# VectorE takes over the output copies of unit 1 in the first network's steps, one core

## The chip, the cores and the metric

One core of a Trainium2 chip runs the whole program. The metric is the time in microseconds (us) from launch to end on the device; the median of several runs counts, and one execution is profiled. TensorE multiplies and transposes into PSUM, whose eight banks are `bank[0]` to `bank[7]` here, each 128 partitions by 512 float32. ScalarE (ACT in the profile) and VectorE (DVE) read PSUM and write SBUF; GpSimd (POOL) works in SBUF alone; SyncE (SP) issues transfers.

## The reference, cut to what matters

```
x = x + cross_attention_0(layernorm(x), ctx)        # 16 heads of 8
x = x + network_0(layernorm(x))                     # 6 layers, 16 heads of 64, windows of 32 tokens
x = x + cross_attention_1(layernorm(x), ctx)
x = x + network_1(layernorm(x))                     # 2 layers, 8 heads of 64, windows of 64 tokens
# one layer of network_0, for each of 16 batches of 128 tokens x 128:
h = shift_tokens(x);  q, k, v = split(h @ Wqkv)
q, k = l2norm(q) * qs, l2norm(k) * ks               # per head
q, k = rotate(q), rotate(k)                         # rotary tables, 8 * cos and sin
p = softmax(mask(q @ k.T));  x = x + (p @ v) @ Wo
x = x + (a * gelu(gate)) @ W2 + b2,   a, gate = split(norm(shift_tokens(x)) @ W1 + b1)
```

All of it is float32 but the mask, which is added in bfloat16.

## The kernel before

Each engine has one program written out by hand, and the engines meet at semaphores: `wait_ge(sem, n)` before an instruction, `then_inc(sem, 1)` behind it. An engine takes its instructions strictly in the order of its program, so one that waits holds up all behind it.

The first network is a pipeline of steps `s = 0 ... 98`. A batch of one layer (`p`, 0 to 95) is split in two units of 8 heads, `i = 0` and `i = 1`. `step_0(s)` exists once for every engine; it works on `p = s` (queries, keys, rotation, sums of squares), on `s - 1` (norm, turning q and k, scores of unit 0), on `s - 2` (softmax, values) and on `s - 3` (values of unit 1, projection by `wo`, residual). The feed-forward network works on groups of four batches and spreads over four steps, which I call by their counter c of `ff_phase`, (s - 7) mod 4: c = 0 mean, variance and the previous group's second matmul, c = 1 normalise and first gate matmul, c = 2 the other gate matmuls, with `ACT.Gelu` on ScalarE at the step's end, c = 3 the hidden matmuls.

What touches the change, in the order of one step:

- TensorE: `values_all(1, s-3)` (line 790) writes the attention output of unit 1 into banks 7 and 6 and increments `AT["o"][1]`. Then `keys(1, s)` and `queries(1, s)` (line 710, two matmul rows each) into banks 1 and 0. Then `project_out` (line 823, 16 rows) waits for `AT["oe"][1]`, reads `o_t[0]` and `o_t[1]` and writes bank 7. Later the values of unit 1 (`project_in(1, s-2, 2, 7, "v")`, line 710) overwrite bank 7 and wait for `AT["res"][0]`, the residual.
- ScalarE: after the squares of unit 0 and `turned(0, s-1, 0)` comes `outputs(1, s-3)`, two copies of 128x256 from banks 7 and 6 into `o_t[1]` (line 1609), then the exponents of unit 1 (line 1578). The same helper copies unit 0's output at the end of the step, before the next step's exponents of unit 0.
- VectorE: newton's last two operations (line 2180 writes `rnorm`), `rotate(0, s, 1)` and `rotate(0, s, 0)`, the reciprocals of the softmax sums, one feed-forward operation, two sums of squares (line 2136), `row_max_all(1, s-2)` (line 2195, two reductions), `rotate(1, s, 1)` and `rotate(1, s, 0)` (lines 2124 and 2129, three instructions each), `residual(0, s-3)` (line 2214), and so on until newton.

The words that tie them:

```
pe.wait_ge(AT["oe"][i], p + 1)         # project_out, for i in (0, 1)
at(pe, AT["res"][0], s - 2)            # before the values of unit 1 go to bank 7
dve.wait_ge(AT["k" if c else "q"], un(i, p))   # rotate: keys or queries are in the bank
```

Of the kernel before, what the change touches and what calls it, by code (L numbers as in the profile page):

```python
# [63 lines left out]
def build(nc, A, out):  # L64
# [9 lines left out]
    with ExitStack() as ctx:  # L74
        sb = lambda name, shape, dt=F32: ctx.enter_context(nc.sbuf_tensor(name, shape, dt))
        sem = lambda name: ctx.enter_context(nc.semaphore(name))
        bank = [ctx.enter_context(nc.psum_tensor(f"bank{i}", [P, BLK], F32)) for i in range(8)]
# [64 lines left out]
        o_t = [slot(34 + i) for i in range(2)]  # L142
# [38 lines left out]
        AT = {n: [sem(f"at_{n}{i}") for i in range(2)] for n in UNIT}  # L181
# [23 lines left out]
        def un(i, p):  # L205

            return 2 * p + i + 1
# [5 lines left out]
        def at(eng, sem_, n):  # L213

            if n > 0:
                eng.wait_ge(sem_, n)

        def ff_phase(ph, s):

            t = s - ph["lo"]  # L220
            first, steps, groups = (7, 4, 24) if ph["net"] == 0 else (5, 2, 8)
            if t < first:
                return -1, -1, -1
            g, c = divmod(t - first, steps)
            f = 4 * ph["layer0"] + g
            return c, f if g < groups else -1, f - 1 if 1 <= g <= groups else -1
# [87 lines left out]
        def g_square(act, n, k):  # L314

            act.wait_ge(LN["cen"], NBLK + n + 1)
            nc.scalar.activation(g_sq[n % 2], g_cen[n % 2], ACT.Square).then_inc(LN["sq"], 1)
# [1133 lines left out]
        def _(act):  # L1451
# [89 lines left out]
            def act_phase(ph):  # L1541
                lo, hi, ni = ph["lo"], ph["hi"], ph["net"]
                live = lambda p: lo <= p < hi

                def square(i, p, c):

                    act.wait_ge(AT["rk" if c else "rq"], un(i, p))
                    at(act, AT["ssk" if c else "ssq"], un(i, p - 1))
                    nc.scalar.activation(sq[i][c], bank[c][:], ACT.Square).then_inc(AT["sqk" if c else "sqq"], 1)  # L1549
# [20 lines left out]
                def exponents_all(i, p):  # L1570

                    at(act, AG["pt"][i][0], p - 1)
                    at(act, AG["ri"][i][0], p - 1)
                    for g in range(2):
                        act.wait_ge(AG["mx"][i][g], p + 1)
                        for j in range(4):
                            h = 2 * j + g
                            ins = nc.scalar.activation(pb[i][0][p % 2][:, h * DH:(h + 1) * DH], bank[3 + g][:, j * DH:(j + 1) * DH],  # L1578
                                                       ACT.Exp, bias=amx[p % 2][:, i, h:h + 1], accum_out=asum[p % 2][:, i, h:h + 1])
                        ins.then_inc(AG["ex"][i][g], 1)  # L1580

                def probs_all(i, p):

                    act.wait_ge(AG["pt"][i][0], p + 1)
                    at(act, AT["o"][i], p)
                    nc.scalar.activation(pbt[i][0], bank[5 + i][:], ACT.Copy).then_inc(AG["pte"][i][0], 1)
# [7 lines left out]
                def values(i, p):  # L1594

                    act.wait_ge(AT["v"][i], p + 1)
                    at(act, AT["o"][i], p)
                    nc.scalar.activation(v_s[i], bank[7][:], ACT.Copy).then_inc(AT["ve"][i], 1)
# [35 lines left out]
                def step_0(s):  # L1634
                    c, f, before = ff_phase(ph, s)
                    if live(s - 2):
                        exponents_all(0, s - 2)
                        values(0, s - 2)
                    if live(s - 3):
                        probs_all(1, s - 3)  # L1640
                    if live(s):
                        square(0, s, 1)
                        square(0, s, 0)
                    if s == 0:
                        gate_weights()
                    if live(s - 1):
                        turned(0, s - 1, 0)
                    if live(s - 3):
                        outputs(1, s - 3)
                    if s in (1, 3, 5):  # L1650
                        g_square(act, (s + 1) // 2, (s + 1) // 2)
                    if c == 0 and f >= 0:
                        ff_square(f)
                    if c == 1 and f >= 0:
                        ff_affine(f)
                    if live(s - 2):
                        exponents_all(1, s - 2)
                    if live(s):
                        square(1, s, 1)
                        square(1, s, 0)  # L1660
                    if live(s - 1):
                        turned(0, s - 1, 1)
                    if s == hi:
                        for k in range(2):
                            g_square(act, 4 + k, k)
                    if live(s - 2):
                        probs_all(0, s - 2)
                        values(1, s - 2)
                    if live(s - 1):
                        turned(1, s - 1, 1)  # L1670
                        turned(1, s - 1, 0)
                    if c == 2 and f >= 0:
                        ff_gelu(f)
                    if live(s - 2):
                        outputs(0, s - 2)
# [148 lines left out]
            t1, outputs = act_phase(PHASES[1])  # L1824
# [209 lines left out]
        def _(dve):  # L2034
# [76 lines left out]
            def dve_phase(ph):  # L2111
                lo, hi, ni = ph["lo"], ph["hi"], ph["net"]
                live = lambda p: lo <= p < hi

                def rotate(i, p, c):
# [15 lines left out]
                                                      ALU.mult)  # L2131
                    ins.then_inc(AT["rk" if c else "rq"], 1)

                def sum_squares(i, p, c):
                    dve.wait_ge(AT["sqk" if c else "sqq"], un(i, p))
                    nc.vector.tensor_reduce(ss[:, i, HU * c:HU * c + HU], heads(sq[i][c]), AX.X, ALU.add  # L2136
                                            ).then_inc(AT["ssk" if c else "ssq"], 1)
# [52 lines left out]
                def row_max_all(i, p):  # L2190

                    dve.wait_ge(AT["s"], un(i, p))
                    for g in range(2):
                        at(dve, AG["ex"][i][g], p - 1)
                        nc.vector.tensor_reduce(amx[p % 2][:, i, g:HU:2], bank[3 + g][:, 0:256].rearrange("p (j k) -> p j k", j=4),  # L2195
                                                AX.X, ALU.max, negate=True).then_inc(AG["mx"][i][g], 1)
# [130 lines left out]
                def step_0(s):  # L2327
                    if live(s - 1):
                        newton(s - 1, 9, 11)
                    if s == hi:  # L2330
                        outer(ph, 0)
                        outer(ph, 1)
                    if live(s):
                        rotate(0, s, 1)
                        rotate(0, s, 0)
                    if s == 0:
                        x_step(NB + 1)
                    if live(s - 2):
                        row_sum_all(0, s - 2)
                    feed_forward_0(s, 0)  # L2340
                    if live(s):
                        sum_squares(0, s, 1)
                        sum_squares(0, s, 0)
                    if live(s - 2):
                        row_max_all(1, s - 2)
                    if live(s):
                        rotate(1, s, 1)
                        rotate(1, s, 0)
                    if live(s - 3):
                        residual(0, s - 3)  # L2350
                    feed_forward_0(s, 1)
                    if s == hi:
                        for k in range(2):
                            g_centre(dve, 4 + k, k, k)
                    if s == hi + 1:
                        for k in range(2):
                            g_normalise(dve, 4 + k, k, k)
                    if live(s - 2):
                        row_sum_all(1, s - 2)
                    if live(s):  # L2360
                        sum_squares(1, s, 0)
                        sum_squares(1, s, 1)
                    feed_forward_0(s, 2)
                    if live(s):
                        newton(s, 0, 3)
                    if live(s - 1):
                        row_max_all(0, s - 1)
                    if live(s):
                        newton(s, 3, 6)
                        newton(s, 6, 9)  # L2370
                    if s == hi:
                        for k in range(2):
                            g_newton(dve, 4 + k, k, k)
# [324 lines left out]
```

## Time and profile before

| what | value |
|---|---|
| three runs | 2305.04 us median, 2299.03 to 2306.47 |
| profiled execution | 2299.02 us, span 2297.2 us, granted clock 0.987 |
| TensorE matmul busy | 2124.9 us, 93% of the span |
| VectorE busy | 1760.9 us, 77% |
| ScalarE busy | 1712.2 us, 75% |
| GpSimd busy | 1340.2 us, 58% |

The span runs from the first to the last instruction; the run's own time is 1.8 us longer. Busy time of TensorE counts matmul rows whose ends are modelled. The steps s = 7 to 94 of the first network fill 256 to 1765 us of the span.

### The profile page before, as it was taken

The numbers are of one execution on the slowest core, as the hardware profiler recorded it, in microseconds if no ns is written. First come the engines' busy times: TensorE is split into PE (matmuls) and PEld (weight loads), VectorE is DVE, ScalarE is ACT, GpSimd is POOL, SyncE is SP. The second block draws the span as 40 slices with busy tenths as digits, with TensorE's granted clock in tenths as the row PEclk, the third lists the DMA queues.
The fourth block names the chain that finished last, engine by engine and source line by source line (L and its number), as shares of the span: only waits on it lengthen the run. The fifth ranks groups of instructions, "written<-read, shape, count | busy, mean of one in ns | idle before, by whom it ended". The sixth has DMA issues, their size and how long they took to land. (4 is left out here: it accounts for less than half of the span.)

```text
span 2297.2 us, 88445 instructions
## 1 busy us (share of the span) xinstructions
PE 2124.9 (93%) x33790; PEld 1456.7 (63%) x33790; DVE 1760.9 (77%) x4953; ACT 1712.2 (75%) x5916; POOL 1340.2 (58%) x1270
## 2 busy tenths in 40 slices
PE   7988999999999999999999999999999886899997
PEld 5656666666666666666666666666666564666665
DVE  4988877778777878777778777877777478788873
ACT  3767788787787877787887777887788543778784
POOL 1337666666666666665676566666666124766660
PEclk8999999999999999999999999999999998999999
DMA  4001221112211222112211122111221100000001
GB/s 112 4 3 39 70 58 45 41 46 67 57 43 39 64 51 57 39 43 61 57 46 42 43 65 60 46 39 45 52 53 43 48 10 10 13 13 16 13 9 28
DMA packets 144799, 96.93 MB, mean 42 GB/s; under 512 B 61976, under 2 KB 137408, under 8 KB 144384
## 3 DMA queue, kind: packets, MB, share of 16 engines
q1 hardware_dynamic: 143232, 91.02, 15.5%
q8 instruction: 274, 4.49, 0.8%
q14 instruction: 141, 1.16, 0.2%
q10 hardware_dynamic: 1152, 0.26, 0.1%
HBM read 23.11 MB, written 1.05 MB: 11 GB/s over the span
## 5 line engine op out<-in xcount | busy, mean ns | idle before, releaser
L710 PE MATMUL bank<-wqkv,hs 128*128 128x512 f32 x1344 | 666.7, 614 | 19.3 <-ACT arena L1609 13.7
L1931 POOL TENSOR_TENSOR arena<-arena,rnorm 128x512 f32<-128x512 f32 x448 | 455.5, 1046 | 388.5 <-DVE rnorm L2180 387.3
L1924 POOL TENSOR_TENSOR arena<-arena 128x512 f32<-128x512 f32 x448 | 568.0, 1275 | 132.5 <-DVE arena L2129 132.2
L1578 ACT ACTIVATE arena<-bank,amx 128x64 f32<-128x64 f32 x1536 | 458.8, 336 | 8.5 <-DVE amx L2195 8.3
L2124 DVE TENSOR_TENSOR arena<-bank,rot 128x512 f32<-128x512 f32 x448 | 306.9, 685 | 82.7 <-PE bank L710 79.0
L1555 ACT ACTIVATE arena<-bank 128x512 f32<-128x512 f32 x448 | 264.4, 617 | 132.0 <-PE bank L731 130.9
L710 PEld LDWEIGHTS bank<-wqkv,hs 128*128 128x128 f32 x1344 | 228.6, 191 | 203.8 <-issue 154.9
L1578 ACT ACTIVATION_READ_ACCUMULATOR arena<-bank,amx 128x1 f32 x1536 | 352.3, 229 | 0.0
L2129 DVE TENSOR_TENSOR arena<-bank,rot 128x256 f32<-128x256 f32 x896 | 334.0, 414 | 0.0
L731 PEld LDWEIGHTS bank<-ident,arena 128*128 128x128 f32 x1792 | 212.6, 142 | 152.8 <-issue 128.3
L2136 DVE TENSOR_REDUCE ss<-arena 128x8 f32<-128x512 f32 x448 | 283.4, 670 | 32.5 <-ACT arena L1549 32.3
L1549 ACT ACTIVATE arena<-bank 128x512 f32<-128x512 f32 x448 | 265.9, 647 | 42.0 <-DVE arena L2129 41.2
L1938 POOL TENSOR_TENSOR arena<-arena,ainv 128x512 f32<-128x512 f32 x192 | 200.7, 1045 | 164.9 <-DVE ainv L2203 164.7
L731 PE MATMUL bank<-ident,arena 128*128 128x128 f32 x1792 | 251.5, 274 | 14.1 <-POOL arena L1931 6.4
L1609 ACT ACTIVATE arena<-bank 128x256 f32<-128x256 f32 x384 | 127.2, 387 | 174.6 <-PE bank L790 173.7
L823 PEld LDWEIGHTS bank<-arena,wo 128*128 128x128 f32 x1792 | 221.6, 194 | 55.1 <-issue 48.1
L790 PE MATMUL bank<-arena 64*64 64x32 f32 (+1 forms) x9216 | 186.1, 221 | 49.0 <-issue 47.6
L823 PE MATMUL bank<-arena,wo 128*128 128x128 f32 x1792 | 226.9, 279 | 3.0 <-ACT arena L1609 2.6
L790 PEld LDWEIGHTS bank<-arena 64*64 64x64 f32 x9216 | 160.6, 134 | 71.0 <-issue 54.5
L2195 DVE TENSOR_REDUCE amx<-bank 128x4 f32<-128x256 f32 x384 | 143.8, 416 | 39.8 <-PE bank L767 39.2
L767 PE MATMUL bank<-arena 64*32 64x64 f32 (+1 forms) x12288 | 168.8, 217 | 0.0
L767 PEld LDWEIGHTS bank<-arena 64*32 64x32 f32 x12288 | 154.9, 105 | 0.3
(213 smaller groups left out, 3229.8 us busy)
## 6 DMA issues: line engine op xcount, KB each, us to landing
arena<-arena SPq DMA_DIRECT2D x768, 64.0 KB
wqkv<-in_L_ffn_Wqkv_dram SPq DMA_DIRECT2D x24, 256.0 KB
hs<-z SPq DMA_DIRECT2D x128, 32.0 KB, 1.8
hs<-z SPq DMA_DIRECT2D x128, 31.8 KB, 1.9
fx<-z SPq DMA_DIRECT2D x31, 128.0 KB, 2.2
fx<-z SPq DMA_DIRECT2D x31, 127.0 KB, 2.5
wqkv<-in_L_ffn_Wqkv_dram SPq DMA_DIRECT2D x24, 128.0 KB
w<-in_L_ffn_W_dram SPq DMA_DIRECT2D x6, 341.0 KB
```

The source lines that it names most:

```text
L710: nc.tensor.matmul(bank[o][:], src[:], wqkv[w][:, off:off + 512], start=True, stop=True).then_inc(AT[name] if part < 2 else AT[name][i], 1)
L731: mm = nc.tensor.transpose(bank4[o][:, j, :], rc[i][c][p % 2][:, j * P:(j + 1) * P], ident[:])
L767: mm = nc.tensor.matmul(bank[3 + g][q:q + 32, DH * j:DH * j + n], q_t[i][rows, P * j + q:P * j + q + 32], k_t[i][rows, P * j + key:P * j + ...
L790: mm = nc.tensor.matmul(bank4[7 - half][to:to + DH, j, q0:q1], src[g][rows, DH * h:DH * h + DH], pbt[i][0][rows, h * P + q0:h * P + q1], s ...
L823: mm = nc.tensor.matmul(bank4[7][:, 0, :], wo[w][:, i, j, :] if ni == 0 else wo[w][:, j // 2, j % 2, :], o_t[i][:, j * P:(j + 1) * P], sta ...
L1549: nc.scalar.activation(sq[i][c], bank[c][:], ACT.Square).then_inc(AT["sqk" if c else "sqq"], 1)
L1578: ins = nc.scalar.activation(pb[i][0][p % 2][:, h * DH:(h + 1) * DH], bank[3 + g][:, j * DH:(j + 1) * DH], ACT.Exp, bias=amx[p % 2][:, i, ...
L1924: nc.gpsimd.tensor_tensor(t, t, rs[i][c], ALU.add).then_inc(AT["ak" if c else "aq"][i], 1)
L1931: nc.gpsimd.tensor_tensor(t, t, rnorm[p % 2][:, i, HU * c:HU * c + HU].unsqueeze(2).to_broadcast([P, HU, DH]), ALU.mult).then_inc(AT["mk" ...
L2124: nc.vector.tensor_tensor(heads(rc[i][c][p % 2]), src, r[:, 2 * c, :].unsqueeze(1).to_broadcast([P, HU, DH]), ALU.mult)
L2129: ins = nc.vector.tensor_tensor(dst, src[:, :, (1 - a) * hd:(2 - a) * hd], r[:, 2 * c + 1, a * hd:(a + 1) * hd].unsqueeze(1).to_broadcast( ...
L2136: nc.vector.tensor_reduce(ss[:, i, HU * c:HU * c + HU], heads(sq[i][c]), AX.X, ALU.add).then_inc(AT["ssk" if c else "ssq"], 1)
```

## The change

VectorE gets a new helper `outputs`, called in its `step_0` between the maxima and the rotation of unit 1, for steps before `hi` = 96. ScalarE leaves its two copies out in those steps and keeps them from step 96 on. Data, banks, matmuls and semaphores stay as they were; TensorE's program is the same.

```diff
@@ ScalarE, step_0 @@
                     if live(s - 1):
                         turned(0, s - 1, 0)
-                    if live(s - 3):
+                    if live(s - 3) and (s >= hi):
                         outputs(1, s - 3)
@@ VectorE, dve_phase @@
+                def outputs(p):
+
+                    dve.wait_ge(AT["o"][1], p + 1)
+                    at(dve, AT["y"][0], p)
+                    for part in range(2):
+                        ins = nc.vector.tensor_copy(o_t[1][:, 256 * part:256 * part + 256], bank[7 - part][:, 0:256])
+                    ins.then_inc(AT["oe"][1], 1)
+
@@ VectorE, step_0 @@
                     if live(s - 2):
                         row_max_all(1, s - 2)
+                    if live(s - 3) and s < hi:
+                        outputs(s - 3)
                     if live(s):
                         rotate(1, s, 1)
                         rotate(1, s, 0)
```

On VectorE, in a step with c = 1, before the change, from the second sum of squares to the residual (`bank1` and `bank0` hold keys and queries of unit 1, `at_` names are the semaphores waited for):

```order
L2136 TENSOR_REDUCE ss<-arena 128x8 [waits at_sqq]
L2195 TENSOR_REDUCE amx0<-bank3 128x4 [waits at_ex10,at_s]
L2195 TENSOR_REDUCE amx0<-bank4 128x4 [waits at_ex11]
L2124 TENSOR_TENSOR arena<-bank1,rot1 128x512 [waits at_ak1,at_kt1,at_k]
L2129 TENSOR_TENSOR arena<-bank1,rot1 128x8x32 x2
L2124 TENSOR_TENSOR arena<-bank0,rot1 128x512 [waits at_aq1,at_qt1,at_q]
L2129 TENSOR_TENSOR arena<-bank0,rot1 128x8x32 x2
L2214 TENSOR_TENSOR z<-bank7,z 128x128 [waits at_y0]
```

The same place of VectorE's program with the change (lines of the maxima are 2203 here, of the residual 2222):

```order
L2144 TENSOR_REDUCE ss<-arena 128x8 [waits at_sqq]
L2203 TENSOR_REDUCE amx0<-bank3 128x4 [waits at_ex10,at_s]
L2203 TENSOR_REDUCE amx0<-bank4 128x4 [waits at_ex11]
L2139 COPY arena<-bank7 128x256 [waits at_y0,at_o1]
L2139 COPY arena<-bank6 128x256
L2124 TENSOR_TENSOR arena<-bank1,rot1 128x512 [waits at_ak1,at_kt1,at_k]
L2129 TENSOR_TENSOR arena<-bank1,rot1 128x8x32 x2
L2124 TENSOR_TENSOR arena<-bank0,rot1 128x512 [waits at_aq1,at_qt1,at_q]
L2129 TENSOR_TENSOR arena<-bank0,rot1 128x8x32 x2
L2222 TENSOR_TENSOR z<-bank7,z 128x128 [waits at_y0]
```

Two copies stand between the maxima and the rotation, and six rotation instructions and the residual stand behind them.

On ScalarE, the same step before the change, from the squares of unit 0 to the exponents of unit 1:

```order
L1549 ACTIVATE arena<-bank1 128x512 [waits at_ssk,at_rk]
L1549 ACTIVATE arena<-bank0 128x512 [waits at_ssq,at_rq]
L1555 ACTIVATE arena<-bank5 128x512 [waits at_s,at_qt0]
L1609 ACTIVATE arena<-bank7 128x256 [waits at_y0,at_o1]
L1609 ACTIVATE arena<-bank6 128x256
L1624 ACTIVATE arena<-arena,lnp0 128x512 [waits ff_xn]
L1578 ACTIVATE arena,asum0<-bank3,amx0 128x64 [waits at_mx10,at_ri10,at_pt10]
```

And with it:

```order
L1549 ACTIVATE arena<-bank1 128x512 [waits at_ssk,at_rk]
L1549 ACTIVATE arena<-bank0 128x512 [waits at_ssq,at_rq]
L1555 ACTIVATE arena<-bank5 128x512 [waits at_s,at_qt0]
L1624 ACTIVATE arena<-arena,lnp0 128x512 [waits ff_xn]
L1578 ACTIVATE arena,asum0<-bank3,amx0 128x64 [waits at_mx10,at_ri10,at_pt10]
```

The two copies and their wait for `at_o1` are gone from between the turned queries and the feed-forward operation.

## Rows read from the trace of the kernel before

**Rows 1.** Page, part 1: busy us, share of the span, instructions

```profile
PE 2124.9 (93%) x33790; PEld 1456.7 (63%) x33790; DVE 1760.9 (77%) x4953; ACT 1712.2 (75%) x5916; POOL 1340.2 (58%) x1270
```

**Rows 2.** Busy by engine from 256 to 1765 us: PE, PEld, DVE, ACT, POOL, PEclk

```profile
256.00:1765.00 1509.00, 1428.99 (x26397) 984.11 (x26397) 1180.93 (x3429) 1203.42 (x4385) 977.51 (x915) 1.00 0.20 50
```

**Rows 3.** Waits of PE, same stretch: us in total, times, longest us

```profile
PE bank L790 <- issue: 41.4, 62, 1.8
PE bank L761 <- issue: 19.4, 22, 1.0
PE bank L710 <- ACT arena L1609: 12.9, 15, 0.9
```

**Rows 4.** Timeline of step 80 (c = 1): start us, us, engine line, [idle before]

```profile
1514.36 0.66 ACT L1609 ACTIVATE arena<-bank 128x256 f32<-128x256 f32 x2 [0.21 <-PE bank L790]
...
1514.79 0.75 DVE L2195 TENSOR_REDUCE amx<-bank 128x4 f32<-128x256 f32 x2
...
1515.45 0.68 DVE L2124 TENSOR_TENSOR arena<-bank,rot 128x512 f32<-128x512 f32 x1
1515.61 0.19 PEld L823 LDWEIGHTS bank<-arena,wo 128*128 128x128 f32 x1 [0.24 <-issue]
...
1516.04 1.95 PE L823 MATMUL bank<-arena,wo 128*128 128x128 f32 x16
...
1518.03 0.29 DVE L2214 TENSOR_TENSOR z<-bank,z 128x128 f32<-128x128 f32 x1
...
1518.59 0.30 PEld L710 LDWEIGHTS bank<-wqkv,hs 128*128 128x128 f32 x2
1518.70 1.02 PE L710 MATMUL bank<-wqkv,hs 128*128 128x512 f32 x2
```

**Rows 5.** Timeline of step 78 (c = 3)

```profile
1480.85 0.74 DVE L2195 TENSOR_REDUCE amx<-bank 128x4 f32<-128x256 f32 x2
...
1481.61 0.19 PEld L823 LDWEIGHTS bank<-arena,wo 128*128 128x128 f32 x1 [0.24 <-issue]
...
1482.04 1.95 PE L823 MATMUL bank<-arena,wo 128*128 128x128 f32 x16
...
1484.03 0.28 DVE L2214 TENSOR_TENSOR z<-bank,z 128x128 f32<-128x128 f32 x1
...
1485.45 0.30 PEld L710 LDWEIGHTS bank<-wqkv,hs 128*128 128x128 f32 x2
```

**Rows 6.** Timeline of step 79 (c = 0)

```profile
1496.00 0.74 DVE L2195 TENSOR_REDUCE amx<-bank 128x4 f32<-128x256 f32 x2
1497.45 0.69 DVE L2124 TENSOR_TENSOR arena<-bank,rot 128x512 f32<-128x512 f32 x1 [0.71 <-PE bank L710]
...
1497.68 0.19 PEld L823 LDWEIGHTS bank<-arena,wo 128*128 128x128 f32 x1 [0.24 <-issue]
```

**Rows 7.** Groups of DVE by shape, 256 to 1765 us: count, busy us, mean ns

```profile
L2129 DVE TENSOR_TENSOR arena<-bank,rot 128x256 f32<-128x256 f32 x704 | 262.4, 414 | 0.0
...
L2252 DVE COPY arena<-bank 128x512 f32<-128x512 f32 x44 | 29.5, 670 | 8.6 <-PE bank L859 8.6
```

**Rows 8.** Timeline of step 78's start: PE released by a copy of ScalarE

```profile
1473.73 0.63 ACT L1609 ACTIVATE arena<-bank 128x256 f32<-128x256 f32 x2
...
1474.41 1.13 PE L710 MATMUL bank<-wqkv,hs 128*128 128x512 f32 x2 [0.86 <-ACT arena L1609]
```

**Rows 9.** Timeline of ACT, step 81 (c = 2), before the Gelu

```profile
1534.57 0.60 ACT L1555 ACTIVATE arena<-bank 128x512 f32<-128x512 f32 x1 [0.69 <-PE bank L731]
```

**Rows 10.** Timeline of steps 8 and 94, first and last of the stretch

```profile
278.67 0.74 DVE L2195 TENSOR_REDUCE amx<-bank 128x4 f32<-128x256 f32 x2
...
279.47 0.19 PEld L823 LDWEIGHTS bank<-arena,wo 128*128 128x128 f32 x1 [0.24 <-issue]
...
1754.57 0.74 DVE L2195 TENSOR_REDUCE amx<-bank 128x4 f32<-128x256 f32 x2
...
1755.34 0.19 PEld L823 LDWEIGHTS bank<-arena,wo 128*128 128x128 f32 x1 [0.24 <-issue]
```

## The prediction, made before the changed kernel had run

> **What bounds the kernel now.** I read the page's busy line first, to see which engine has no room. TensorE is busy for 93% of the span, VectorE 77% and ScalarE 75% [rows 1]. Then the windows: over the first network's steps TensorE is busy for 1428.99 of 1509.00 us at full clock, with 1180.93 for VectorE and 1203.42 for ScalarE [rows 2]. Only about 80 us are left in which TensorE does nothing, so the next question is who makes it wait. The waits answer it: 41.4 us inside the values matmuls and 19.4 us before the masks end with "issue", and 12.9 us end with ScalarE's output copy [rows 3]. Line 790 has no semaphore between its rows, so its stalls are of TensorE's own instruction stream. The 22 waits at line 761 and the 15 at line 710 come in steps with c = 3, behind the Gelu. Two of these three groups are therefore the only idle time that a lighter ScalarE could give back, and everything else that delays a TensorE instruction is paid in full.
>
> **What the change removes.** It takes 93 pairs of copies from ScalarE, 0.66 us a pair [rows 4]. Does anyone wait for that? The relief would have to reach the Gelu at the end of a step with c = 2, since what TensorE waits for comes behind it. Between the copy and the Gelu stands line 1555, before which ScalarE is idle for 0.69 us, until TensorE has turned the keys [rows 9]. I see such an idle time in each of the steps with c = 2 that I looked through (eight, from step 9 to 93). Freed time becomes more of that idle time. I count the removal as 0; the cover is TensorE's own order, and if it were gone the gain would be at most 0.66 us in each of 22 steps.
>
> **What it adds to VectorE.** Two copies of 128x256 out of PSUM. The nearest row is line 2129: the same shape, 414 ns each, the two of a pair 0.75 us from first start to last end [rows 7, 4]. The first of such a pair begins 0.34 us ahead of the second (0.75 less 0.41). The copy of 128x512 takes 670 ns [rows 7], less than two of the half size. So I take 0.66 us for what follows on VectorE and 0.75 us until `AT["oe"][1]` is incremented. Lower bound: the one copy of double width, 0.67 us, less the 0.09 by which the next instruction overlaps (the maxima end at 1515.54, the rotation starts at 1515.45 [rows 4]): 0.58. Upper bound: two of 414 ns without overlap, 0.82.
>
> **Where it lies beside other work.** In a step with c = 0 (and, from the same reading, c = 2), the maxima end at 1496.74, and the rotation starts 0.71 us later because it waits for the keys [rows 6]. Copies of 0.66 us fit. They end at 1496.66 + 0.75 = 1497.41, and TensorE loads `wo` at 1497.68: 0.2 us to spare. Cost 0.
>
> In a step with c = 1 or 3 VectorE is late: the maxima end at 1515.54 (1514.79 + 0.75) and the rotation starts at once, at 1515.45 [rows 4]. ScalarE had begun to copy at 1514.36, so the output has long been ready. Now the copies start at 1515.45 and end at 1516.20. TensorE wants to load `wo` at 1515.61 and to multiply at 1516.04. How a release that is late is paid is shown by [rows 8]: copies end at 1474.36, the next matmul row starts at 1474.41, and the pair takes 1.13 us instead of the 1.02 of [rows 4]. So 0.05 us for the semaphore and 0.11 us of an uncovered weight load. The projection effectively starts at 1516.20 + 0.16 = 1516.36 instead of 1516.04: 0.32 us late. For c = 3: the maxima end at 1481.59, the copies at 1482.26, the start moves to 1482.42 instead of 1482.04: 0.38 us [rows 5].
>
> **What is late next.** Behind the copies on VectorE stand both rotations and the residual, which TensorE needs before it puts the next values into bank 7. For c = 1: from the first rotation to the residual it is 2.58 us (1515.45 to 1518.03), of which the last 0.05 may be the projection's own end (1516.04 + 1.95 = 1517.99), so 2.53. From 1516.11 on that gives 1518.64, and 0.29 for the residual 1518.93, plus 0.16: the values start at 1519.09 instead of 1518.70 [rows 4]. That is 0.39 us, which contains the 0.32, not in addition. For c = 3 the residual ended at 1484.31 and the values are loaded at 1485.45 [rows 5], so 0.66 us more is hidden. The squares, sums and newton behind it follow TensorE again: the next gate copy waits for its matmul in any case. TensorE's delay moves the next step as a whole, and nothing later in it catches up.
>
> **How many steps.** I compared the end of the maxima with the load of `wo` in all steps from 4 to 95. The pattern of the rows above holds from step 8 (279.41 against 279.47) to step 94 (1755.31 against 1755.34) [rows 10]: 17 steps with c = 3, and 14 with c = 1 in which the residual comes out 0.4 to 0.5 us late (mean 0.45), and steps 4 and 6 like them. In the other 5 and 8 TensorE was itself late, mostly by a stall of its instructions, and the copies find room.
>
> Sum: 17 x 0.38 = 6.5, 14 x 0.45 = 6.3, 2 x 0.45 = 0.9: 13.7 us, say 14. Against the profiled execution's own time, 2299.02, that is 2313. The three runs have their median 6 us above that execution and their mean at 2303.5; I put the 14 us on the mean and forecast 2317 us. With the lower bound (0.58, 0.08 less in 33 steps) it is 11 us, with the upper (0.82, 0.16 more) 19.
>
> **A rule beside a row.** The row of line 2129 shows that the second of two instructions without a wait between them starts before the first has ended, 0.34 us after its start [rows 4, 7]. The Trainium skill ("VectorE: DVE Perf Modes", "The DRAIN you can't avoid") says that the next operation does not start until the pipe is empty, while its section on two Vector instructions with no wait between them lets one that is not held start earlier; its cost table gives 120 + 256 cycles at 0.96 GHz for one copy out of PSUM, 0.39 us, 0.78 for two. By the first rule with that price each of 33 steps would lose 0.12 us more and the sum would be an estimated 18 us. The rows decide for the overlap.
>
> **Rivals.**
> 1. *The copies are hidden* (0 to 6 us, about 2304). If TensorE's stalls of "issue" [rows 3] run on their own time, waiting 0.4 us earlier in a step lets its instructions arrive, and the stall shrinks by as much. For it: 41.4 us of such stalls, one in every second step. Against it: they come several us away from the projection. To bring 14 us under 6, over half would have to be absorbed.
> 2. *ScalarE's relief decides* (faster, about 2293). Place: the Gelu at the end of c = 2. ScalarE loses the copies and the idle time in front of them, 0.66 + 0.21 = 0.87 us in [rows 4]. If the 0.69 us of [rows 9] were ScalarE's own lateness seen through TensorE, the Gelu would start earlier by that much, and the 32.3 us of waits behind it [rows 3] would shrink by 22 x 0.87 = 19 us, at most by all 32. Against it: the idle time before line 1555 in every such step. It decides from 14 / 22 = 0.64 us a step on; 19 to 32 us back against 14 lost gives 2299 to 2285.
> 3. *The margin of c = 0 and 2 goes too.* It is 0.2 us. If a copy takes 0.6 us instead of 0.41 (two banks, the wait on `AT["o"][1]`), the pair costs 1.1, 0.44 more: 33 steps lose 0.44 more, and the 44 others 0.2: 14 + 14.5 + 9 = 37 us, 2341. Nothing in the rows speaks for it but that no such pair stands in them.
>
> **Chances.** Forecast (10 to 20 us more) 0.70; rival 1 0.17; rival 2 0.06; rival 3 0.07. About 0.3%, 7 us, is what a measurement of this kernel can tell from no change. The range 2302 to 2331 leaves out rival 2, most of rival 3 and the lower part of rival 1; the forecast's own is 2309 to 2325. Slower is the forecast and rival 3, 0.77; within 0.3% rival 1, 0.17; faster 0.06.
>
> **What would show it.** In the profile after: ACT's line 1609 falls from 384 to 198 rows; DVE has 186 copies of 128x256 near 0.41 us; a new line in TensorE's waits, the projection or its weight load released by VectorE's copy, about 0.3 us each in some 30 steps, and the values of unit 1 released by the residual with c = 1; steps with c = 1 and 3 longer by 0.4 us, the others unchanged; ScalarE's idle time before line 1555 with c = 2 still there. I am wrong if the step lengths with c = 1 and 3 stay (rival 1), if the waits behind the Gelu shrink (rival 2) or if the steps with c = 0 and 2 grow (rival 3).

## The result: 13 us slower, and where the profile shows it

| what | before | with the change |
|---|---|---|
| six runs each, median | 2302.77 us (2299.03 to 2306.47) | 2315.49 us (2312.96 to 2323.08) |
| profiled execution | 2299.02 us, span 2297.2 us, clock 0.987 | 2314.1 us, span 2311.8 us, clock 0.987 |

The ratio is 1.0061, 95% interval 1.0047 to 1.0075: 11 to 17 us, 14 by the ratio and 13 by the medians. The forecast was 2317.

The busy line of the page with the change, against [rows 1]:

```profile
PE 2132.2 (92%) x33790; PEld 1450.2 (63%) x33790; DVE 1824.2 (79%) x5139; ACT 1670.9 (72%) x5730; POOL 1340.3 (58%) x1270
```

VectorE has 186 instructions more and 63 us more work, ScalarE 186 fewer and 41 us less. TensorE's count is the same, and it is the engine that the time follows. What it waits for in the first network's steps (256 to 1780 us; us in total, times, longest), against [rows 3]:

```profile
PE bank L790 <- issue: 41.6, 59, 2.1
PE bank L761 <- issue: 18.9, 22, 1.0
PE bank L710 <- ACT arena L1609: 12.8, 15, 0.9
PE bank L823 <- DVE arena L2139: 6.2, 29, 0.6
```

The three old groups stand where they stood. One is new: the projection waits 29 times for VectorE's copy. The other sign that the prediction named for c = 1, the values of unit 1 released by the residual, is not there: neither TensorE's matmuls nor its weight loads have a row that ends with line 2222 in this stretch. What ScalarE waits for in the same stretch is the other half of the story:

```profile
ACT arena L1555 <- PE bank L731: 121.9, 133, 2.4
ACT arena L1609 <- PE bank L790: 84.0, 65, 2.4
ACT arena L1549 <- DVE arena L2129: 77.9, 126, 2.3
ACT arena L1578 <- DVE amx L2203: 58.9, 88, 1.2
```

Before, the same view (256 to 1765 us) had these rows:

```profile
ACT arena L1609 <- PE bank L790: 156.0, 131, 4.3
ACT arena L1555 <- PE bank L731: 117.7, 133, 2.2
...
ACT arena L1549 <- DVE arena L2129: 14.4, 43, 1.1
ACT arena L1578 <- DVE amx L2195: 4.5, 18, 0.5
```

ScalarE no longer waits 72 us for unit 1's values; it waits 64 us more for the rotated keys and queries and 54 us more for the maxima. So here ScalarE, which follows the others, does not get further when work is taken from it; it waits at the next place. Part of these waits is due to VectorE, which now comes 0.66 us later; e6 below shows the relief alone.

The steps themselves. Step 78 (c = 3) with the change; start us, duration us, engine and line, idle time before and its releaser in brackets; compare [rows 5]:

```profile
1493.58 0.74 DVE L2203 TENSOR_REDUCE amx<-bank 128x4 f32<-128x256 f32 x2
...
1494.24 0.74 DVE L2139 COPY arena<-bank 128x256 f32<-128x256 f32 x2
...
1494.90 0.68 DVE L2124 TENSOR_TENSOR arena<-bank,rot 128x512 f32<-128x512 f32 x1
1495.09 1.86 PEld L823 LDWEIGHTS bank<-arena,wo 128*128 128x128 f32 x16 [0.99 <-DVE arena L2139]
1495.12 2.02 PE L823 MATMUL bank<-arena,wo 128*128 128x128 f32 x16 [0.20 <-DVE arena L2139]
...
1497.42 0.28 DVE L2222 TENSOR_TENSOR z<-bank,z 128x128 f32<-128x128 f32 x1
...
1498.61 0.30 PEld L710 LDWEIGHTS bank<-wqkv,hs 128*128 128x128 f32 x2
```

From the start of the maxima to the projection it was 1482.04 - 1480.85 = 1.19 us and is 1495.12 - 1493.58 = 1.54: 0.35 later. The projection itself is 0.07 longer (2.02 for 1.95); its first weights are now loaded 0.03 before it, where before they were loaded 0.43 ahead, beneath an earlier matmul. Note that the wait in brackets says only 0.20 us for these 0.42. The list of waits above (6.2 us in 29 times) therefore understates what the release costs; the distance between two instructions tells it. The residual is early in both (1484.03 before the load at 1485.45; 1497.42 before 1498.61).

Step 80 (c = 1), against [rows 4]:

```profile
1527.95 0.74 DVE L2203 TENSOR_REDUCE amx<-bank 128x4 f32<-128x256 f32 x2
...
1528.61 0.75 DVE L2139 COPY arena<-bank 128x256 f32<-128x256 f32 x2
...
1529.27 0.68 DVE L2124 TENSOR_TENSOR arena<-bank,rot 128x512 f32<-128x512 f32 x1
...
1529.47 1.86 PEld L823 LDWEIGHTS bank<-arena,wo 128*128 128x128 f32 x16 [0.93 <-DVE arena L2139]
1529.50 2.02 PE L823 MATMUL bank<-arena,wo 128*128 128x128 f32 x16
...
1531.79 0.28 DVE L2222 TENSOR_TENSOR z<-bank,z 128x128 f32<-128x128 f32 x1
...
1532.12 0.30 PEld L710 LDWEIGHTS bank<-wqkv,hs 128*128 128x128 f32 x2
1532.23 1.02 PE L710 MATMUL bank<-wqkv,hs 128*128 128x512 f32 x2
```

From maxima to projection 1.25 us before, 1.55 now; from maxima to residual 3.24 and 3.84; from maxima to the values' matmul 3.91 and 4.28, 0.37 later. These 0.37 are the projection's: it starts 0.30 later and is 0.07 longer, and from its end to the values' matmul it is 0.71 us both times (1517.99 to 1518.70, 1531.52 to 1532.23), two groups of transposes without a gap. The residual ends at 1532.07, 0.05 before the values' weights are loaded. Its release has used up its margin but holds nothing up.

Step 79 (c = 0), against [rows 6]:

```profile
1509.89 0.74 DVE L2139 COPY arena<-bank 128x256 f32<-128x256 f32 x2
...
1510.62 0.69 DVE L2124 TENSOR_TENSOR arena<-bank,rot 128x512 f32<-128x512 f32 x1
1510.85 0.19 PEld L823 LDWEIGHTS bank<-arena,wo 128*128 128x128 f32 x1 [0.24 <-DVE arena L2139]
...
1511.28 1.95 PE L823 MATMUL bank<-arena,wo 128*128 128x128 f32 x16
```

The copies end at 1510.63, 0.22 us before the load, and load and matmul stand 0.43 apart, as in [rows 4]. The bracket names VectorE's copy, but its 0.24 us is the same idle time that "issue" ended before: the last releaser of a wait isn't always its reason.

I took a step's length as the time from its first rotation to the next step's. From steps 7 to 94, 22 of each c, the median change is +0.33 us with c = 1, +0.44 with c = 3, and 0.00 and 0.01 with c = 0 and 2. Steps 4 and 6 are 0.90 and 0.96 longer, but in the profile with the change the clock stood at its lower level at the end of step 6 (granted clock 0.96 over that step, 1.00 in the one before). At full clock step 6 is only about 0.2 longer.

### The profile page after: what moved, and what is told of

The parts are those of the page before. It is cut to its first block and busy times, and to the rows that moved or that the text cites. A ratio compares the mean times of both kernels' runs of the same rounds, so it can differ in the third digit from the quotient of the medians.

```text
span 2311.8 us, 88445 instructions
## 1 busy us (share of the span) xinstructions
PE 2132.2 (92%) x33790; PEld 1450.2 (63%) x33790; DVE 1824.2 (79%) x5139; ACT 1670.9 (72%) x5730; POOL 1340.3 (58%) x1270
## 5 line engine op out<-in xcount | busy, mean ns | idle before, releaser
L710 PE MATMUL bank<-wqkv,hs 128*128 128x512 f32 x1344 | 673.6, 620 | 19.2 <-ACT arena L1609 13.6
L1555 ACT ACTIVATE arena<-bank 128x512 f32<-128x512 f32 x448 | 262.5, 613 | 135.5 <-PE bank L731 134.3
L1549 ACT ACTIVATE arena<-bank 128x512 f32<-128x512 f32 x448 | 270.8, 634 | 107.3 <-DVE arena L2129 107.3
L1578 ACT ACTIVATION_READ_ACCUMULATOR arena<-bank,amx 128x1 f32 x1536 | 341.9, 223 | 0.0
L1598 ACT ACTIVATE arena<-bank 128x512 f32<-128x512 f32 x224 | 139.5, 623 | 18.6 <-PE bank L710 18.4
```

The source lines that it names most:

```text
L710: nc.tensor.matmul(bank[o][:], src[:], wqkv[w][:, off:off + 512], start=True, stop=True).then_inc(AT[name] if part < 2 else AT[name][i], 1)
```

## The experiments

Each was timed beside the kernel before on its own chip. **Time at full clock** below is the mean over the runs of a kernel of span x granted clock. TensorE bounds this kernel, so this is about what it would take if the clock never fell. It is my estimate from two numbers of each run, and it spreads less (standard error 0.4 to 0.9 us) than the times do (1.0 to 2.8 us).

| run | ratio to before, 95% | median us, this / before | at full clock, us over before | clock, this / before |
|---|---|---|---|---|
| e1_odd_steps | 1.0002 (0.9987 to 1.0018) | 2303.97 / 2301.26 | +0.5 | 0.9849 / 0.9850 |
| e2_even_steps | 1.0056 (1.0034 to 1.0078) | 2316.67 / 2301.26 | +12.9 | 0.9848 / 0.9850 |
| e3_before_maxima | 1.0057 (1.0036 to 1.0077) | 2315.15 / 2301.26 | +11.0 | 0.9840 / 0.9850 |
| e4_added_work | 1.0147 (1.0124 to 1.017) | 2337.2 / 2301.26 | +28.6 | 0.9828 / 0.9850 |
| e5_after_key_rotation | 1.0623 (1.0588 to 1.0658) | 2446.68 / 2301.79 | +139.9 | 0.9840 / 0.9852 |
| e6_light_scalare | 0.9997 (0.9979 to 1.0014) | 2301.44 / 2301.79 | -1.1 | 0.9850 / 0.9852 |
| e7_unit0_on_vectore | 0.997 (0.9955 to 0.9985) | 2296.7 / 2301.79 | -12.7 | 0.9822 / 0.9852 |
| e8_reductions_after_maxima | 1.0047 (1.0026 to 1.0068) | 2316.5 / 2302.23 | +4.9 | 0.9819 / 0.9848 |
| e9_reductions_before_maxima | 1.0053 (1.003 to 1.0075) | 2315.42 / 2302.23 | +6.2 | 0.9828 / 0.9848 |

The kernel with the change has 2279.5 us at full clock, against 2265.7 for the kernel before as timed beside e1 to e4, on another chip: +13.8. (The clocks of the kernel before beside the change itself are not on record.)

**e1_odd_steps and e2_even_steps: which steps pay.** e1 keeps VectorE's copies only in steps with odd s (c = 0 and 2), e2 only in those with even s (c = 1 and 3).

```diff
@@ e1, against the changed kernel; e2 has the parities the other way @@
-                    if live(s - 3) and (s >= hi):
+                    if live(s - 3) and (s >= hi or s % 2 == 0):
                         outputs(1, s - 3)
...
-                    if live(s - 3) and s < hi:
+                    if live(s - 3) and s < hi and s % 2 == 1:
                         outputs(s - 3)
```

> VectorE makes unit 1's output copies only in odd steps (c = 0 and 2), ScalarE in even ones. Theory A (the loss is the late release of the projection and, with c = 1, of the residual, in steps where VectorE has no idle time before the rotation): all of the loss is gone, same as before within 3 us (about 2303). Theory C (the copies cost in any step, through contention or longer work of VectorE): about half of the 13 us stays, 2309.

> VectorE makes the copies only in even steps (c = 1 and 3). Theory A: the whole loss, 12 to 15 us over before, about 2316. Theory C: half of it, about 2309.

e1 takes the time of the kernel before, e2 that of the whole change. e2's median steps are +0.33 (c = 1) and +0.44 (c = 3), the others 0.00 and -0.02. So the 44 or so pairs with c = 0 and 2 are free, and the cost is all in the other half. e1 tells one thing more: in its steps with c = 2 ScalarE is rid of the two copies and of the wait in front of them, at no cost elsewhere, and the waits behind the Gelu stay as they were (18.7 and 12.9 us in its list, 19.4 and 12.9 in [rows 3]). That is the test of rival 2 in its own place.

**e3_before_maxima: release early, residual late.** The copies move in front of the maxima. They end earlier, so the projection isn't held up, but everything behind stays 0.66 us late.

```diff
@@ against the changed kernel, VectorE, step_0 @@
-                    if live(s - 2):
-                        row_max_all(1, s - 2)
                     if live(s - 3) and s < hi:
                         outputs(s - 3)
+                    if live(s - 2):
+                        row_max_all(1, s - 2)
```

> All copies on VectorE, but ahead of the maxima, so that they end some 0.66 us earlier while the rotation and all behind it are as late as in the changed kernel. Theory A: the projection is released in time; only the residual with c = 1 stays late, 14 steps by 0.4 us, 5 to 7 us over before (2309). Theory B (VectorE's lateness as such costs, through squares, sums and newton): the whole 13 us stays, 2316. The waits of the projection for VectorE should be nearly gone in A.

The matmuls' wait for VectorE's copy is gone from the list. 30 weight loads still wait for it, but the projection starts 1.75 us behind the end of line 790's matmuls in the median step of each c, as in the kernel before, so they cost nothing. Yet the run is 11 us over before, not 5 to 7. That was a miss, and left a question: do late maxima cost something, or do the copies? See e9.

**e4_added_work: the delay without the copies, in the wrong size.** ScalarE keeps its copies, and VectorE gets two unused products in their place.

```diff
@@ against the kernel before, VectorE, step_0, between row_max_all(1, s - 2) and rotate(1, s, 1) @@
+                    if live(s - 3) and s < hi:
+                        for part in range(2):
+                            nc.vector.tensor_tensor(spare[:, part], rot_c[0][:], rot_c[1][:], ALU.mult)
```

> The kernel before, ScalarE keeps all copies, and VectorE makes two unused products of 128x256 in SBUF (about 0.7 us) between the maxima and the rotation. Theory A: no late projection, only the late residual with c = 1, 5 to 7 us over before (2309). Theory B: 13 us (2316). If ScalarE's relief was worth something in the changed kernel, this one is slower than that.

Far above both theories. The group of these products on VectorE (count | busy us, mean ns | idle before), and two pairs of them in the timeline, the second (step 80) with GpSimd beside it, say why (lines are one higher here):

```profile
L2349 DVE TENSOR_TENSOR spare<-rot_c 128x256 f32<-128x256 f32 x174 | 143.9, 866 | 0.0
```

```profile
1510.13 0.75 DVE L2349 TENSOR_TENSOR spare<-rot_c 128x256 f32<-128x256 f32 x2
...
1544.41 1.84 DVE L2349 TENSOR_TENSOR spare<-rot_c 128x256 f32<-128x256 f32 x2
1544.75 1.22 POOL L1939 TENSOR_TENSOR arena<-arena,ainv 128x512 f32<-128x512 f32 x1
1545.93 1.46 POOL L1925 TENSOR_TENSOR arena<-arena 128x512 f32<-128x512 f32 x1
```

While GpSimd was idle a pair took 0.75 us, beside a running GpSimd instruction 1.84. In the median step a pair took 0.75 us with c = 3 and 1.92 us with c = 0, 1 and 2. So the dose was the 0.66 us of the change in steps with c = 3, and nearly three times that in the others. The Trainium skill ("SBUF — State Buffer", "Who interferes with whom") says that a VectorE instruction with two SBUF inputs contends with a GpSimd instruction that reads SBUF, and that such contention is an exclusive lock. This trace agrees with it, 1.84 beside 0.75 us.

What the run still tells is where such a delay is paid. With c = 3, where the dose was right, the median step is +0.04 us, against +0.44 with the change: VectorE's lateness without the late release costs nothing there. With c = 0 and 2 even the large dose is free (0.00 and +0.01). With c = 1 it is +1.51. TensorE's waits name the place, line 711 being the matmul of the values of unit 1 into bank 7 and line 2215 the residual:

```profile
PE bank L711 <- DVE z L2215: 19.7, 16, 1.4
```

**e8_reductions_after_maxima and e9_reductions_before_maxima: the right size.** A reduction with one input from SBUF takes the place of the product; e8 puts the two behind the maxima, e9 in front.

```diff
@@ e8, against e4; e9 has the three lines ahead of row_max_all(1, s - 2) @@
-                            nc.vector.tensor_tensor(spare[:, part], rot_c[0][:], rot_c[1][:], ALU.mult)
+                            nc.vector.tensor_reduce(spare[:, part], rot_c[0][:], AX.X, ALU.max)
```

> The kernel before with two unused reductions of 128x256 (of a table in SBUF, one input) on VectorE between the maxima and the rotation of unit 1, in the steps where the change puts its copies; ScalarE keeps its copies. The reductions stand where the two products of the run with added work stood, but a reduction of this shape takes about 0.42 us as the maxima do, a pair 0.74 us, so this is the dose of the change, 0.66 us. Theory A (two releases): the projection waits for ScalarE and starts in time, so c = 3 costs nothing; with c = 1 the residual is late by what the change makes it, 0.3 to 0.4 us: 14 to 17 steps, 5 to 7 us in all. Rival B (VectorE's lateness as such costs a step, through maxima, squares and newton too): 13 us, in c = 1 and c = 3 alike. Rival C (the work that ScalarE keeps has to be counted as well): over 13 us.

> As the run before in this call, but the two reductions stand in front of the maxima of unit 1 instead of behind them. This repeats on VectorE what the run with the copies before the maxima did, without moving any copy. That run was 12 to 13 us over the kernel before where theory A gave 5 to 7. If late maxima are the reason (the exponents of unit 1 on ScalarE start later, and with them the transposes and values of unit 1), this run is 10 to 13 us over the kernel before and the one with the reductions behind the maxima 5 to 7. If the reason lies with the copies themselves (their wait for the values of unit 1 holds up maxima and rotation in some steps), both runs are equal within 3 us, at 5 to 7.

In e8 the dose is right. Step 76 (c = 1) with reductions, projection, residual and the values' matmul (line 711), and, below it, the group:

```profile
1457.66 0.73 DVE L2349 TENSOR_REDUCE spare<-rot_c 128x4 f32<-128x256 f32 x2
1457.80 0.19 PEld L824 LDWEIGHTS bank<-arena,wo 128*128 128x128 f32 x1 [0.24 <-issue]
...
1458.23 1.95 PE L824 MATMUL bank<-arena,wo 128*128 128x128 f32 x16
...
1460.83 0.28 DVE L2215 TENSOR_TENSOR z<-bank,z 128x128 f32<-128x128 f32 x1
...
1461.16 0.30 PEld L711 LDWEIGHTS bank<-wqkv,hs 128*128 128x128 f32 x2 [0.35 <-DVE z L2215]
1461.16 1.12 PE L711 MATMUL bank<-wqkv,hs 128*128 128x512 f32 x2
```

```profile
L2349 DVE TENSOR_REDUCE spare<-rot_c 128x4 f32<-128x256 f32 x176 | 64.6, 408 | 0.0
```

The projection starts in time, released by ScalarE, and now the residual is what TensorE waits for: from the projection's end (1460.18) to the values' matmul it is 0.98 us in place of 0.71. The median step is +0.32 us with c = 1 and +0.09 with c = 3, and the time at full clock is +4.9 us: theory A in place and size. By the clock on the wall it is 11 us over before (1.0047, interval 6 to 16 us), which the 13 us of rival B would fit as well; what speaks for A are the steps and the time at full clock. The rest is the granted clock, 0.9819 on the mean of 12 runs against 0.9848 in 20: 0.0029 x 2300 = 7 us. e9 equals e8 within the errors, at full clock as well (+6.2). So late maxima are not what made e3 dear; the 5 us between e3 and e9 go with the copies themselves, as e9's expectation had it. In e3 VectorE is seen to wait for the values before its copies, and maxima and rotation stand behind that wait:

```profile
DVE arena L2139 <- PE bank L790: 37.2, 54, 1.7
```

That this wait makes the whole 5 us is argued, not shown. Beside it stands that e3's list has 45.9 us of stalls at line 790, 4.5 more than before (e8 43.4, e9 44.6), and no run tells the two apart.

**e5_after_key_rotation: the release later still.** The copies move behind `rotate(1, s, 1)`.

```diff
@@ against the changed kernel, VectorE, step_0 @@
+                    if live(s):
+                        rotate(1, s, 1)
                     if live(s - 3) and s < hi:
                         outputs(s - 3)
                     if live(s):
-                        rotate(1, s, 1)
                         rotate(1, s, 0)
```

> All copies on VectorE, behind the rotation of the keys of unit 1, 1.27 us later than in the changed kernel. Theory A: each us by which the projection is released late costs a us in every step: about 1.6 us in 31 steps with c = 1 and 3, 1.5 us in the 59 others, 140 us over before (2440, 2400 to 2460). Theory B: VectorE's program is as long as in the changed kernel, so about 2316.

Measured +145 us. Every step pays, +1.58, 1.63, 1.56 and 1.69 us for c = 0 to 3, and the wait has grown:

```profile
PE bank L823 <- DVE arena L2139: 114.1, 87, 1.8
```

The projection's release is thus a hard edge. Once the 0.2 us of margin with c = 0 and 2 are used up, each step pays the delay in full.

**e6_light_scalare: what ScalarE's relief is worth.** The kernel before, with ScalarE's two copies cut to one of 8 columns. The wait for the values of unit 1 in front of the copy stays, and two thirds of the 0.66 us go.

```diff
@@ against the kernel before, ScalarE, outputs @@
-                    if ni == 0:
+                    if ni == 0 and i == 1 and 2 <= p < 93:
+                        nc.scalar.activation(o_t[1][:, 0:8], bank[7][:, 0:8], ACT.Copy).then_inc(AT["oe"][1], 1)
+                    elif ni == 0:
```

> The kernel before with ScalarE copying only 8 columns of one bank for unit 1, in place of two copies of 256 columns (batches 2 to 92 of the pipeline), so that most of unit 1's attention output is left out of the projection: ScalarE's relief alone, about 0.45 us a step. Theory A: no gain, 2303 within 3 us, because ScalarE waits for TensorE before line 1555. Rival (the relief counts): up to 10 us faster, 2293.

Ratio 0.9997, and at full clock -1.1 us with a standard error of 0.8. Relief of this copy is worth nothing that can be told from zero. Where the freed time went, with VectorE's program as it was (against the list of before above, line 1608 being the small copy):

```profile
ACT arena L1555 <- PE bank L731: 126.5, 134, 2.4
ACT arena L1611 <- PE bank L790: 83.6, 65, 2.2
ACT arena L1608 <- PE bank L790: 67.7, 63, 2.5
ACT arena L1549 <- DVE arena L2131: 30.0, 51, 1.1
...
ACT arena L1578 <- DVE amx L2197: 14.3, 26, 0.7
```

It is 9 us more before line 1555, 16 more for the rotations and 10 more for the maxima.

**e7_unit0_on_vectore: the copy for which TensorE does wait.** [rows 3] has 12.9 us of waits for ScalarE's copy, and [rows 8] shows one: unit 0's, behind the Gelu. This kernel leaves unit 1's copies with ScalarE and gives VectorE unit 0's, in steps with c = 2 only, in the idle time between newton's operations.

```diff
@@ against the kernel before; ScalarE, end of step_0 @@
-                    if live(s - 2):
+                    if live(s - 2) and not (c == 2 and f >= 0):
...
@@ VectorE, between newton(s, 3, 6) and newton(s, 6, 9); outputs_0 is as outputs, of unit 0 @@
+                    if live(s - 2) and c == 2 and f >= 0:
+                        outputs_0(s - 2)
```

> The kernel before, but in the 24 steps with c = 2 the output copies of unit 0 behind the Gelu go to VectorE, between two thirds of newton. If the waits at lines 710 and 761 with c = 3 come from ScalarE's chain behind the Gelu, they shrink by the 0.63 us of the copies: 22 to 24 steps, 13 us faster, about 2290. If VectorE's later newton holds up the norm on GpSimd and the turned queries, the gain is eaten, 2300 to 2305.

It is faster than both kernels: 2296.7 us in 12 runs, ratio 0.997. The waits of 12.9 us have become 0.8, while those before the masks grew from 19.4 to 25.0 (some of the gain meets the next late thing):

```profile
PE bank L790 <- issue: 40.3, 64, 2.0
PE bank L761 <- issue: 25.0, 19, 1.6
PE bank L731 <- POOL arena L1931: 4.8, 15, 0.8
PE bank L710 <- issue: 1.2, 2, 1.0
PE bank L710 <- ACT arena L1609: 0.8, 1, 0.8
```

VectorE has room for the pair here:

```profile
1533.11 0.76 DVE L2139 COPY arena<-bank 128x256 f32<-128x256 f32 x2 [0.71 <-PE bank L790]
```

At full clock it gains 12.7 us, the 13 expected. On the wall it gains 5 to 7, less than expected (2290), since its granted clock is 0.9822 against 0.9852.

## Why the prediction came out right

**Removal counted as 0.** Right. e1 shows it in the steps with c = 2, wait included, and e6 shows most of it alone in all steps. The lists of ScalarE's waits show where the freed time went: not only into the idle time before line 1555, as I wrote (9 us in e6, 4 with the change), but mostly into waits for rotations and maxima. The 0.69 us before line 1555 of [rows 9] is 0.45 in the same step with the change. Still there, and by e1 rival 2 had nothing to win.

**Price of the pair.** 0.66 us to the next instruction and 0.74 to 0.75 to the release: in step 78 they start at 1494.24 and the rotation at 1494.90. The mean of one copy is 413 ns in 186. The overlap that [rows 4, 7] showed for line 2129 holds for copies too. By the rule of the Trainium skill ("VectorE: DVE Perf Modes", "The DRAIN you can't avoid") without overlap the sum was 18 us. The 0.66 us from the first copy to the rotation, under two times 0.413, decide against it here; the total of 14 alone would not, since it came together partly by luck, as follows.

**c = 0 and 2 free.** Right, by e1 and by 0.22 us of margin left in step 79; e5 shows what lies beyond it.

**c = 3, 17 x 0.38.** The mechanism is right (e2 against e8: the median +0.44 becomes +0.09 once ScalarE releases). The term was a little small, 0.44 for 0.38. In step 78 it is 0.42: the copies end at 1494.98 and the projection starts 0.14 later, for which I had 0.05, and it is 0.07 longer, for which I had 0.11.

**c = 1, 14 x 0.45.** Here the number is near and the mechanism is half right. I let the residual decide (0.39 in step 80, with the projection's 0.32 inside it). Measured are 0.37 in step 80, all of it the late and longer projection; in none of the 22 steps is there a gap between it and the values' matmul. The residual arrives just in time, and the wait for it that I had named as a sign did not come. Alone it would cost nearly as much: in e8, where the projection is in time, the median step is +0.32, against +0.33 in the change. Before the change it had 0.33 us of margin (it ended at 1518.32, the values' matmul began at 1518.70, and a release takes 0.05), and 0.66 less 0.33 is what e8 pays; e4 pays 1.83 less 0.33 = 1.5. So the two releases run out together, and to repair only one of them would gain little in these steps, as e3 shows (+0.39).

**Steps 4 and 6, 0.45 each.** I had no closer reading of them than "like the others". At full clock they cost 0.90 and about 0.2, together 1.1 for 0.9, in one execution of each kernel.

The sum of all step lengths at full clock (each step's length less half of the time that the clock spent at its lower level, from one profile of each kernel) is 13.8 us longer from step 0 to 95: 9.3 with c = 3, where I had 6.5; 4.8 with c = 1, where I had 6.3; 1.3 less with c = 0, 0.0 with c = 2, and 1.0 in steps 0 to 6. 18 steps with c = 3 and 13 with c = 1 are over 0.2 us longer, for the 17 and 14 that I had counted. Such sums scatter by the stalls of TensorE's instructions: in e1, where nothing is to be seen, the four differ from before by -1.5 to +1.3 us. So the count of steps is borne out, c = 3 was sized too small, and that the forecast sum of 13.7 came so near is partly luck. By the profiles' own clock the same stretch is 18.9 us longer; 5 us of this is TensorE's clock, at its lower level for 24 us of it with the change and for 14 before.

**Rival 1** (stalls absorb the delay) fell: 41.4 us of issue stalls at line 790 before, 41.6 after. **Rival 3** fell with e1.

## What to carry to other kernels

Ask of an operation that is to move who waits for its release, and who waits for what will stand behind it, and price both in every kind of step: the same two copies cost nothing in half of the steps and 0.33 to 0.44 us in the others. Where two releases run out at the same time, a list of waits names only one of them, and an experiment that restores the other alone shows the second. Relief of an engine that itself waits in every step was worth nothing here; look in TensorE's waits for the one copy that it waits for (here unit 0's behind the Gelu) and move that one. To measure a suspected delay, fill it with an instruction whose duration is known in that place, not with one that may compete with another engine.

## What the runs showed of the hardware that I had not expected

- The same VectorE product of two SBUF tiles (128x256 each) took about 0.42 us with GpSimd idle and 0.87 on the mean over 174, against 0.408 for a reduction of one such tile in the same place. GpSimd's addition of 128x512 was stretched too, to 1.46 us from a mean of 1.28 in the kernel before.
- The mean granted clock depends on the kernel in a way that I can explain only in part. Seven sets of runs lie at 0.984 to 0.985 (all three of the kernel before, e1, e2, e6 and the change), e7 and e8 at 0.982, with standard errors of 0.0005 to 0.0008; e3, e4, e5 and e9 lie between. e7 has 6 us more waits before the masks in the list shown, e8's list differs from before's by under 3 us in each of its three large groups. This took back 7 of e7's 12.7 us and more than doubled e8's loss. In the profiles of before, the change, e7 and e8 each fall of the clock from step 7 to 94 (2, 5, 6 and 7 of them) stands within 2 us of a stall of 1.4 to 2.2 us in TensorE's own instructions, at line 790 or, in e7, also at 761. But each profile has 12 to 14 stalls over 1.2 us at line 790 alone, so most bring no fall. These are single executions; e1's has 6 falls too, one of them with only a stall of 0.6 us before it. Why the mean clock of e7 and e8 is lower than that of e1 or e2 stays open.
- The releaser that a trace names is the last semaphore. With the change 65 idle times of TensorE's weight loads, 39.6 us, are put down to VectorE's copy, but the matmuls wait for it 29 times, 6.2 us.
